# Both head pairs of a narrow score step in one unit, and maximum units of the first row block packed into the third's banks

## The chip, the cores and the metric

The kernel runs on one core of a Trainium2 chip. The metric is the device time of that core in microseconds (us). TensorE is called PE here, VectorE DVE, ScalarE ACT, GpSimd POOL, SyncE SP; PEld is PE's weight load, which the profile lists as a row of its own.

## The reference

One decoder layer with a post-layernorm, on x of 4 batches x 1,024 tokens x 256 channels, 16 heads of 16 channels:

```
x = layernorm(x + causal_self_attention(x))            # q, k, v, o with biases; softmax(q k^T / 4)
x = layernorm(x + cross_attention(x, ctx, mask))        # 64 keys per batch
x = layernorm(x + bitlinear_ffn(x))                     # 1,024 hidden, silu(gate) * up, down;
                                                        # activations to 8 bits, weights to -1, 0, 1
```

The change touches the causal self-attention alone: the scores of each head (queries x keys, keys up to the query's own), their row maximum, and the exponentials.

## The kernel before, in words

**Tiling.** The 1,024 queries of a batch fall into two column blocks c = 0 and 1 of 512 queries, the 16 heads into four groups g of four heads, and a group into two pairs p. The two heads of a pair lie in rows 0 to 63 and 64 to 127 of q_stack and k_stack (float16, each value split into a high and a low part), so that PE multiplies them at the same time. Each of the two writes a PSUM bank of 512 floats per partition. There are eight banks: bank 7 sums the outputs, and banks 0 to 6 are lent to units of work.

**Maximum units** (max_unit on PE, take_max on DVE). Before the exponentials the row maximum of the scores is taken: for a row block of 128 queries (qb, eight per batch, four per column block) PE multiplies queries by keys up to the diagonal, adds minus 1e30 above the diagonal with small matmuls of causal and pick_h, and DVE reduces both banks to the maximum. In column block 0 a (batch, c, g) has six units: row block 0 (128 keys, both pairs side by side in a bank), row block 1 (256 keys, both pairs), row block 2 (384 keys, a unit for each pair) and row block 3 (512 keys, a unit for each pair). Column block 1 has eight units of 512 earlier keys and then the same six. Over 4 batches and 4 groups these are 320 units. After the last one DVE makes the shift of that (c, g), which SP writes as a further row into q_stack.

**Score steps** (scores on PE, exponentials on ACT). A step is one (c, g) and one block kb of 128 keys, now with keys on the partitions and queries along the columns. Steps on the diagonal leave out the queries before their keys, and so have 512, 384, 256 and 128 queries; the others have 512. Every step is two units, one for each pair: two matmuls into two banks, and one exponential of ACT from both banks into probs. There are 192 steps and 384 such units; 32 steps have 256 queries and 32 have 128. On the diagonal POOL then zeroes the upper triangle (the "causal" step, line 727), and PE multiplies probs by v_aug (outputs, line 1069), 8 matmuls a step, into bank 7.

**What sets the order.** All five engines walk one list, `order`, which is spelled out by hand in the string ORDER: a letter takes the next unit of a chain and the digits behind it name the banks it gets. a is a score unit (or a causal step), m a maximum unit, o an output step, r projections, p, h, u and v what comes after the attention (output projection, cross-attention, feed-forward), z a "stir", four filler matmuls of PE. Each engine does its part of the units strictly in this order. A unit's PE part begins with free(u), which waits until the units that last had these banks have been read. When its last matmul ends it raises a semaphore (scores_ready, max_scores, unit_ready), on which the reader waits. probs_ready is raised by ACT, and max_taken by DVE. In this text a *unit boundary* is the place in PE's queue between the last matmul of a unit and the first of the next.

**Lines.** 1031 and 1038 are the score and the mask matmuls of a maximum unit, 1054 those of a score unit, 1069 the output step, 1175 the exponential, 1434 the maximum on DVE, 848, 861 and 928 float32 projections, 1001 and 1013 the feed-forward, 812 the stirs.

Of the kernel before, what the change touches and what calls it, by code (L numbers as in the profile page):

```python
# [15 lines left out]
P = 128  # L16
# [34 lines left out]
    "rr6r0r1ssr2r3r6r0sgsggr6swm01m23m45m01m23z6fm45gr6z1m12m45z3z6fm01m23r6a45m01m23fr6m45fa01fw2ffw3aa45a01w6aa"  # L51
    "45a23am01a45m23a56m01aa56fm23oa01fm45om23aa01z6m45a01m23fowoowm01m45m23sr6m45m01aa23a23aa56m23m01ggo45r6m23m"
    "01oa34aa56a23m01som56a34m12ooom56a34z0xz0m01o23xa56ffoa01m23m45sz6a01m23z6a56m01oa23m56a01oaa23m45m01a23am56"
    "owm23m01a56oga34m56aa12oa01aa23w6m45m01m56m34oowoa01z2z5a56o34a01oa56m23a01om56a23a01om23a45z6m01z6m56m34wz2"
    "a01az5z6a56a34az1z2a56a01oraa23a01m56m34aa12oa56am01oa23m45r6a01aooa34m56z2oa01aa34z2go01m23m45r6rm23m01r4m5"
    "6a23aa01oa34am56om01a23ooom45a23m01arz6z6m23m45wa01r6a01aa45o23om01m56a23oz4aa01em23ogogm45orm01a23r6o01a23m"
    "45obm01p23z5z5a01a45m23p6m45m23a01p6a23a01prm45r6m01em23oz5m01a45opp23m01m45rz6m01m23p6m01a45m23p6pp4p1p2p3g"
    "poaca45a01ap6z2p2p3p4a56a01agoa23a56aa01p4oa23p04a23r6p01p24m01rr6rbp01p23p45m01z6z3p45a23p01z6z6m34p56m01oo"
    "om23m45m01p6p3o01a45oa23a01pm45pr6m01a23m45oa01m23a56oppaa01z2a45am23om01ppa45a23rr6m45aa23p01om23a01aa45p6p"
    "0p1gm45m23oooom45m23p0p1p6p4p5p1p0pa23ar4a01pppp5p6z2o01a45aa23oga45pm01pppap23p6r4a01a56m23aa01a45p6opaa01a"  # L60
    "23z6ppm45pp01p6p3p2pz6z5gm01aa45a23apr6m23a45pa01pop45m01p6p23m45m01oop6p4o23axa01a56ooppa01m34p56ooom01m23m"
    "45p6m01a23p4pa01a23o56ota01oa34m01m56ooa01m23pp56m01m23m45ep6m23m01xa45p6pm45aa01a23p6p0p1gp4paa23a56aom23a0"
    "1a56ap4a01p5a23p6p4om23a01p6oooa45p02z6rr4r6p01p24rr6p01p45p23o01oa56p01p23oa01m45p23z6m01m45p6m45a01m23rp6p"
    "a45a01om56a34aom01m23a56pom56a01m23z4aa01a56aa01a23aa56pa01am23oom45m23ppa01pr6m45m01a23p56oom23m01aa45p6z2b"
    "m23gm45p0p1p6m23m01m45p6p2p3p0rp6o12a45p3pr0aa45a23apppp1p6m45ga23a01ppooooam01m45oa23rr6ro01ppp23p5p6pa01aa"
    "23a45oaa23a01pppm45m23p01p6p4p5paa01a23oooogpppm01m45p23p6o01om23p45p6m01a23a45p6ppp0p1a45a23p6p45om23m45a01"
    "p6p3a12a45r0ppm12m56a34om01aa34om34a01p56om01m23aa45p6m01m45m23p6pp4a01ap5a23p6a01p4gpaa23m01oa45m23a01p6p4p"
    "5a23ooop6a01a23o45p6om45p02rm45om45p01p24r6p01p23gp45m01a23p45p01a23rm56p01m23om45a01m23p6m01p4pm23a01aa56r4"
    "m01a56paoa23a01m56otappea01a23aa56a01m23pproom45m01aa23r6a45m23p01om45m23m01p6r4m23m01p6p4ap5p2p6m34m01p5ggo"
    "p2p3p4a56o01oopa01aa23a45appxpp6p0a23a45bppr6ppp01m23p4p6oooaa23a01pppm45r6o01app23p4p6p5pa34a01oaa23a56aa01"  # L70
    "ppm23gm45pop01p6m23m45p01p6m23a01p4ppp56a23tooxom01m45p6m23a01p4a23o01a56ppoa01m23a56om01a56a23aroa01a56om23"
# [14 lines left out]
    "6h0hooobh6h3oo01h6h3u01v56h3u4uuh05v4vu23h01h24vu6h01h23h45uu0u1v23h45uu6u1h23v0u6h23u05vv4v2h3u04vv2v6h3v6v"  # L86
    "05u23v05hu23u01hhv23hu56v12v34u6hhuuv01h56v0vh1h0uh4vvuuh3h6h2h1h0h5uh4u34hhhhh5h0hu3u1u5hvu6u0u4vhhh23h5h0v"
    "v56uuuhhuu3hhh12h5h0h4u3v5v2v0v4hhhhuv6v3h01h4uvuuh23u01vvvv6v2vu56vvh4h3vv56hu4u1uv56v3hv4z5z2vuz4z2z4z1z4z"
    "5z0z6z3vz0tttz2z4z1"
)  # L90


# [1424 lines left out]
```

## Time and profile before

| | us |
|---|---|
| median of 3 runs (lowest, highest) | 836.62 (831.83, 839.51) |
| the profiled execution | 836.75 |
| its span in the profile | 835.0 |
| PE matmuls busy | 787.4 (94%) |
| DVE busy | 682.5 (82%) |
| ACT busy | 575.8 (69%) |
| POOL busy | 347.6 (42%) |

Busy time is the union of an engine's instructions. A matmul's duration holds its passage through the array besides its columns, and matmuls overlap in it. So the start of the next matmul, not the end of this one, tells what a matmul costs PE. The spaces between columns that are shorter than this passage don't show as idle time. "issue" in the chain of waits is time in which the engine waited for nothing that the profile shows.

### The profile page before, as it was taken

The page shows a single profiled execution, that of the slowest core. Times are in us where ns is not written, and L with a number is a line of the kernel's source. Part 1 is how long each engine was busy: PE and PEld are TensorE (multiplying, and loading weights), DVE is VectorE, ACT ScalarE, POOL GpSimd, SP SyncE. Part 2 cuts the span into 40 slices and gives each one's busy share as a digit, 9 for nine tenths or more (in the row PEclk, how much of TensorE's full clock was granted, in tenths as well). Part 3 has the DMA queues.
Part 4 walks back from the last instruction along what each step waited for, and adds up shares of the span by engine and source line. Part 5 has one row for each costly group of instructions (what it writes and reads, how often), then busy time and mean ns, then how long its engine had stood idle before and what let it go on. Part 6 is the DMA issues. An engine that isn't in the chain of part 4 may idle for free.

```text
span 835.0 us, 20197 instructions
## 1 busy us (share of the span) xinstructions
PE 787.4 (94%) x7444; PEld 387.5 (46%) x7470; DVE 682.5 (82%) x1254; ACT 575.8 (69%) x753; POOL 347.6 (42%) x587
## 2 busy tenths in 40 slices
PE   8889999999999999999999999999999999999878
PEld 6534444354553435434553444544435343545536
DVE  6989998678987899868999589984999759745597
ACT  2457865559856598565876769765796589865495
POOL 5744355333433255423454153551525222652244
PEclk9989999999999999999999999999999999999899
DMA  6433002100212011011022010011101000000001
GB/s 191 125 103 98 2 20 66 54 18 17 67 36 64 1 33 28 3 38 51 13 73 77 1 48 19 8 35 50 46 2 37 11 1 26 26 28 1 2 1 53
DMA packets 37235, 32.86 MB, mean 39 GB/s; under 512 B 9828, under 2 KB 33348, under 8 KB 37140
## 3 DMA queue, kind: packets, MB, share of 16 engines
q1 hardware_dynamic: 33796, 28.89, 12.4%
q0 software_dynamic: 1440, 1.48, 0.8%
q10 hardware_dynamic: 1904, 1.18, 0.6%
q8 instruction: 64, 1.05, 0.6%
q14 instruction: 31, 0.25, 0.1%
HBM read 14.55 MB, written 4.19 MB: 22 GB/s over the span
## 4 chain that ended last, share of the span: by engine, by line
PE 65%; DVE 16%; ACT 9%; issue 6%; POOL 4%; DMA 0%; ACTq 0%; POOLq 0%; DVEq 0%
PE ps L1069 11%; PE ps L848 9%; PE ps L1054 7%; PE ps L1031 6%; DVE shift L1434 6%; PE ps L861 6%; PE ps L928 3%; ACT probs L1175 3%; PE ps L1001 3%; PE ps L1013 2%; PE ps L812 2%; PE ps L958 2%; PE ps L970 2%; PE ps L837 2%; PE ps L953 2%
## 5 line engine op out<-in xcount | busy, mean ns | idle before, releaser
L1175 ACT ACTIVATE probs<-ps 128x1024 f32<-128x1024 f32 (+3 forms) x384 | 294.7, 810 | 120.8 <-PE ps L1054 118.7
L1434 DVE TENSOR_REDUCE shift<-ps 128x2 f32<-128x1024 f32 (+2 forms) x320 | 343.5, 1112 | 42.1 <-PE ps L1031 20.7
L1069 PE MATMUL ps<-probs,v_aug 128*32 128x512 f32 (+3 forms) x1536 | 157.8, 501 | 0.0
L727 POOL TENSOR_SCALAR_AFFINE_SELECT probs<-probs 128x512 f32<-128x512 f32 x128 | 80.2, 637 | 157.9 <-ACT probs L1175 155.5
L1054 PE MATMUL ps<-q_stack,k_stack 49*128 49x512 f16 (+3 forms) x768 | 116.7, 328 | 12.0 <-ACT probs L1175 4.3
L1031 PE MATMUL ps<-k_stack,q_stack 48*128 48x512 f16 (+3 forms) x768 | 112.2, 329 | 9.8 <-DVE shift L1434 4.4
L1054 PEld LDWEIGHTS ps<-q_stack,k_stack 49*128 49x128 f16 x768 | 38.8, 93 | 106.5 <-ACT probs L1175 40.5
L1031 PEld LDWEIGHTS ps<-k_stack,q_stack 48*128 48x128 f16 x768 | 36.1, 94 | 98.4 <-ACT probs L1175 34.8
L1069 PEld LDWEIGHTS ps<-probs,v_aug 128*32 128x32 f32 x1536 | 35.3, 108 | 37.5 <-issue 26.7
L1310 DVE TENSOR_REDUCE shift<-ps 128x8 bf16<-128x512 f32 x64 | 40.1, 683 | 14.2 <-PE ps L939 14.0
L1257 DVE RECIPROCAL rden<-ps 128x16 f32<-128x16 f32 x64 | 16.1, 252 | 41.9 <-PE ps L837 41.5
L1038 PE MATMUL ps<-causal,pick_h 64*128 64x64 bf16 (+1 forms) x768 | 47.6, 198 | 0.0
L787 POOL TENSOR_SCALAR xt<-xt,mean_off,rstd 128x256 f32<-128x256 f32 x84 | 45.5, 554 | 2.3
L779 POOL TENSOR_SCALAR mean_off<-mv 128x4 f32<-128x4 f32 x21 | 4.1, 196 | 100.5 <-DVE mv L1356 100.4
L1038 PEld LDWEIGHTS ps<-causal,pick_h 64*128 64x128 bf16 x768 | 37.9, 95 | 12.9 <-issue 0.5
L1116 ACT ACTIVATE full<-ps,bias_scaled,kq_scale 128x512 f32<-128x512 f32 x30 | 23.4, 780 | 28.5 <-PE ps L861 20.8
L706 POOL CAST part_sb<-full 128x512 f16<-128x512 f32 x28 | 17.0, 609 | 59.8 <-ACT full L1116 59.7
L1307 DVE TENSOR_TENSOR xt<-ps,xt 128x512 f32<-128x512 f32 x32 | 22.0, 688 | 18.7 <-PE ps L848 18.3
L1332 DVE SCALAR_TENSOR_TENSOR region<-ps,dq_u,region 128x512 f32<-128x512 f32 x48 | 33.9, 745 | 1.0 <-PE ps L1001 0.8
L1346 DVE BATCH_NORM_STATS2 stats<-xt 128x6 f32<-128x256 f32 x96 | 34.0, 414 | 0.8
L1134 ACT ACTIVATE region<-ps 128x1024 f32<-128x1024 f32 x24 | 23.3, 1021 | 15.8 <-PE ps L958 15.8
L708 POOL TENSOR_TENSOR part_sb<-full,part_sb 128x512 f16<-128x512 f32 x28 | 32.4, 1157 | 2.3
(241 smaller groups left out, 1372.7 us busy)
## 6 DMA issues: line engine op xcount, KB each, us to landing
q_stack<-part_sb SPq DMA_DIRECT2D x164, 32.0 KB, 2.0
k_stack<-part_sb SPq DMA_DIRECT2D x147, 32.0 KB, 2.0
xT<-in_x_cols SPq DMA_DIRECT2D x8, 512.0 KB, 4.6
xt<-in_x SPq DMA_DIRECT2D x8, 512.0 KB, 3.6
out_x<-xt SPq DMA_DIRECT2D x7, 512.0 KB, 3.0
q_stack<-shiftT SPq DMA_DIRECT2D x128, 1.0 KB
k_stack<-part_sb POOLq DMA_DIRECT2D x45, 32.0 KB, 2.2
region<-in_w_gate SPq DMA_DIRECT2D x4, 256.0 KB, 3.8
```

Of the source, the lines that this page charges most:

```text
L727: pool.affine_select(out=blk, in_=blk, compare_op=ALU.is_ge, fill=0.0, base=0, pattern=[[0, HG], [1, P]], channel_multiplier=-1).then_inc( ...
L787: pool.tensor_scalar(xt[:, t, :], xt[:, t, :], mean_off[:, t:t + 1], rstd[:, t:t + 1], ALU.add, ALU.mult).then_inc(normed, 1)
L848: mm = pe.matmul(ps[:, u.bank, i * C:(i + 1) * C], src[:, d, i * P:(i + 1) * P], w[:, d, :], start=(d == 0), stop=(d == CC - 1))
L861: mm = pe.matmul(ps[:, u.bank, :], (wk, wq)[t][:, d, e * P:(e + 1) * P], xT[:, h, d, :], start=(d == 0), stop=(d == CC - 1))
L1031: mm = pe.matmul(ps[:, u.banks[s], j * w:(j + 1) * w], q_stack[at, u.b % 2, c, h, qb % TH * P:(qb % TH + 1) * P], k_stack[at, u.b % 2, h, ...
L1038: mm = pe.matmul(ps[:, u.banks[s], 0:n * w].rearrange("p (j w) -> p j w", j=n)[:, :, to], pick_h[rows, at], causal[rows, keys].unsqueeze(1 ...
L1054: mm = pe.matmul(ps[:, u.banks[i], 0:BANK - off], k_stack[at, b % 2, h, kb * P:(kb + 1) * P], q_stack[at, b % 2, c, h, off:BANK], start=Tr ...
L1069: mm = pe.matmul(ps[DV * i:DV * (i + 1), SUM_BANK, off:BANK], v_aug[:, kb, at:at + DV], probs_of(b, n)[:, i, :], start=first, stop=last)
L1175: act.activation(probs_of(b, n)[:, 2 * p:2 * p + 2, :], pair(u)[:, :, 0:BANK - off], ACT.Exp, scale=exp_scale).then_inc(probs_ready, 1)
L1310: ins = dve.tensor_reduce(shift2[:, t, e * HC:(e + 1) * HC], ps[:, k, :].rearrange("p (h k) -> p h k", k=TK), AX.X, ALU.max, negate=True)
L1346: ins = dve.bn_stats(stats[:, t, :], xt[:, t, :])
L1434: dve.tensor_reduce(to[:, :, pairs[0]:pairs[-1] + 1, qb % TH], pair(u)[:, :, 0:len(pairs) * w].rearrange("p j (h w) -> p j h w", w=w), AX. ...
```

## The change

Three edits. (1) A score step of 256 or 128 queries becomes one unit: its four matmuls write both pairs side by side into the two banks, and ACT takes them in one exponential. The 32 steps of 256 and the 32 of 128 queries have one unit in place of two, so the score units are 320 where they were 384. The counts of the semaphores stay as they were: such a unit raises scores_ready and probs_ready by two. (2) The maximum unit of the first row block of a column block (128 keys) is dropped; its two pairs are put behind the two pairs of the third row block (384 keys), which leave 128 columns of their banks free. The second row block comes first, the third with the first next, the fourth last. A column block thus has five such units in place of six (288 units where there were 320). DVE takes a packed unit with two reductions, since they have different widths and targets; the two mask matmuls of such a unit and row half reach over both parts. (3) ORDER is written anew: 1,885 entries in place of 1,981; the filler units are 56 in both.

```diff
--- before.py
+++ after.py
@@ -48,45 +48,42 @@
 PARTS, LAST_PARTS = [(0, 4), (4, 4)], [(0, 4), (4, 2), (6, 2)]
 
 ORDER = (
...
 )
 
 
@@ -172,17 +169,31 @@
             at += size
 
 
-    max_units = {0: [], 1: []}
-    for qb in range(TB):
-        w = (qb + 1) * P
-        c, k0 = qb // TH, qb // TH * BANK
-        n = min(BANK // (w - k0), HG // 2)
-        if c > 0:
-            max_units[c] += [(qb, 0, BANK, [p], False) for p in range(HG // 2)]
-        max_units[c] += [(qb, k0, w - k0, list(range(p, p + n)), True) for p in range(0, HG // 2, n)]
+    max_units = {}
+    for c in range(QC):
+        t0 = c * TH
+
+        def diagonal(t, pairs, at):
+            return [(t0 + t, c * BANK, (t + 1) * P, p, True, at + n * (t + 1) * P) for n, p in enumerate(pairs)]
+
+        max_units[c] = [[(t0 + t, 0, BANK, p, False, 0)] for t in range(TH if c > 0 else 0) for p in range(HG // 2)]
+        max_units[c] += [diagonal(1, [0, 1], 0)]
+        max_units[c] += [diagonal(2, [p], 0) + diagonal(0, [p], 3 * P) for p in range(HG // 2)]
+        max_units[c] += [diagonal(3, [p], 0) for p in range(HG // 2)]
+
+    def reductions(unit):
+
+        same = {}
+        for piece in unit:
+            same.setdefault(piece[0], []).append(piece)
+        return list(same.values())
 
     def maxima(b, c, g):
         return [Unit("max", b, (c, g, i), "dve") for i in range(len(max_units[c]))]
+
+    def score_pairs(b, n):
+
+        return [[0, 1]] if BANK - steps[b][n][3] <= BANK // 2 else [[0], [1]]
 
     def crossing():
         return [Unit("maskin", 0, 0)]
@@ -266,7 +277,7 @@
               "f": [Unit("ffn_load", 0, (n, i)) for n in range(3) for i in range(QUARTERS)], "h": [], "x": [], "e": [], "b": [], "c": [], "t": [], "u": [], "v": [], "z": [Unit("stir", 0, n) for n in range(STIRS)]}
     for b in range(NB):
         for n, (g, c, kb, off, diag, begins, ends) in enumerate(steps[b]):
-            chains["a"] += [Unit("scores", b, (n, 0)), Unit("scores", b, (n, 1))] + ([Unit("causal", b, n)] if diag else [])
+            chains["a"] += [Unit("scores", b, (n, pairs[-1])) for pairs in score_pairs(b, n)] + ([Unit("causal", b, n)] if diag else [])
             chains["o"] += [Unit("pv", b, n)] + ([Unit("o_copy", b, n), Unit("turn", b, (c, g), "dve")] if ends else [])
         for c, g in GROUP_ORDER if b < NB - 1 else LAST_ORDER:
             chains["m"] += maxima(b, c, g)
@@ -1016,44 +1027,53 @@
 
             def max_unit(u):
                 c, g, i = u.idx
-                qb, k0, w, pairs, diag = max_units[c][i]
+                unit = max_units[c][i]
                 free(u)
                 if (u.b, i) == (0, 0):
                     pe.wait_ge(consts_ready, 1)
                 if i == 0:
                     for n in (2 * c, 2 * c + 1):
                         wait_moved(pe, u.b, g, n)
-                n = len(pairs)
-                for j, p in enumerate(pairs):
+                masked = unit[0][4]
+                for n, (qb, k0, w, p, diag, to) in enumerate(unit):
                     h = g * HG // 2 + p
                     for s, rows in enumerate(four):
                         at = slice(rows.start, rows.start + SH)
-                        mm = pe.matmul(ps[:, u.banks[s], j * w:(j + 1) * w], q_stack[at, u.b % 2, c, h, qb % TH * P:(qb % TH + 1) * P],
-                                       k_stack[at, u.b % 2, h, k0:k0 + w], start=j == 0 or not diag, stop=not diag)
-                if diag:
+                        mm = pe.matmul(ps[:, u.banks[s], to:to + w], q_stack[at, u.b % 2, c, h, qb % TH * P:(qb % TH + 1) * P],
+                                       k_stack[at, u.b % 2, h, k0:k0 + w], start=n == 0, stop=not masked)
+                if masked:
+                    ends = [to + w for qb, k0, w, p, diag, to in unit]
+                    n, apart = len(unit), ends[-1] - ends[0]
                     for part in range(2):
                         at, keys = slice(part * P, (part + 1) * P), slice(part * HALF, (part + 1) * HALF)
-                        to = slice(w - P + part * HALF, w - HALF + part * HALF)
+                        first = ends[0] - P + part * HALF
                         for s, rows in enumerate(four):
-                            mm = pe.matmul(ps[:, u.banks[s], 0:n * w].rearrange("p (j w) -> p j w", j=n)[:, :, to], pick_h[rows, at],
-                                           causal[rows, keys].unsqueeze(1).broadcast_to([HALF, n, HALF]), start=False, stop=part == 1)
+                            if n == 1:
+                                to, which = ps[:, u.banks[s], first:first + HALF], causal[rows, keys]
+                            else:
+                                to = ps[:, u.banks[s], ends[1] - 2 * apart:ends[1]].rearrange("p (j w) -> p j w", j=2)
+                                to = to[:, :, apart - P + part * HALF:apart - HALF + part * HALF]
+                                which = causal[rows, keys].unsqueeze(1).broadcast_to([HALF, n, HALF])
+                            mm = pe.matmul(to, pick_h[rows, at], which, start=False, stop=part == 1)
                 mm.then_inc(max_scores, 1)
 
             def scores(u):
                 b, (n, pair) = u.b, u.idx
                 g, c, kb, off, diag, first, last = steps[b][n]
+                w, pairs = BANK - off, next(some for some in score_pairs(b, n) if some[-1] == pair)
                 free(u)
                 if first and pair == 0:
                     s = shift_of[b, c, g]
                     pe.wait_ge(shift_loaded[s % 2], 16 * HG * (s // 2 + 1))
                 if (b, n, pair) == (0, 0, 0):
                     pe.wait_ge(ones_moved, 32)
-                h = g * HG // 2 + pair
-                for i, rows in enumerate(four):
-                    at = slice(rows.start, rows.start + SH + 1)
-                    mm = pe.matmul(ps[:, u.banks[i], 0:BANK - off], k_stack[at, b % 2, h, kb * P:(kb + 1) * P],
-                                   q_stack[at, b % 2, c, h, off:BANK], start=True, stop=True)
-                mm.then_inc(scores_ready, 1)
+                for j, p in enumerate(pairs):
+                    h = g * HG // 2 + p
+                    for i, rows in enumerate(four):
+                        at = slice(rows.start, rows.start + SH + 1)
+                        mm = pe.matmul(ps[:, u.banks[i], j * w:(j + 1) * w], k_stack[at, b % 2, h, kb * P:(kb + 1) * P],
+                                       q_stack[at, b % 2, c, h, off:BANK], start=True, stop=True)
+                mm.then_inc(scores_ready, len(pairs))
 
             def outputs(b, n):
                 g, c, kb, off, diag, first, last = steps[b][n]
@@ -1170,10 +1190,16 @@
                 if (n, p) == (0, 0):
                     act.wait_ge(unscale_ready, b + 1)
                     act.reg_load(exp_scale, unscale[0:1, b:b + 1].bitcast(I32))
-                if p == 0 and probs_over[b, n] is not None:
+                pairs = next(some for some in score_pairs(b, n) if some[-1] == p)
+                m, w = len(pairs), BANK - off
+                if pairs[0] == 0 and probs_over[b, n] is not None:
                     act.wait_ge(pv_done, probs_over[b, n] + 1)
-                act.activation(probs_of(b, n)[:, 2 * p:2 * p + 2, :],
-                               pair(u)[:, :, 0:BANK - off], ACT.Exp, scale=exp_scale).then_inc(probs_ready, 1)
+                if m == 1:
+                    to, src = probs_of(b, n)[:, 2 * p:2 * p + 2, :], pair(u)[:, :, 0:w]
+                else:
+                    to = probs_of(b, n).rearrange("p (j s) q -> p j s q", s=2)
+                    src = pair(u)[:, :, 0:m * w].rearrange("p s (j q) -> p j s q", j=m)
+                act.activation(to, src, ACT.Exp, scale=exp_scale).then_inc(probs_ready, m)
 
             exp_scale = act.alloc_register("exp_scale")
             act.dma_start(wk[:], Wk.rearrange("(c p) n -> p c n", p=P)).then_inc(kq_loaded[1], 16)
@@ -1426,14 +1452,17 @@
 
             def take_max(u):
                 c, g, i = u.idx
-                qb, k0, w, pairs, diag = max_units[c][i]
+                unit = max_units[c][i]
                 first = shift[:, c, g, :, :].rearrange("p k (j h t) -> p k j h t", j=2, t=TH)
                 dve.wait_ge(max_scores, u.ready)
                 m = shift_of[u.b, c, g]
-                to = first[:, k0 // BANK]
-                dve.tensor_reduce(to[:, :, pairs[0]:pairs[-1] + 1, qb % TH],
-                                  pair(u)[:, :, 0:len(pairs) * w].rearrange("p j (h w) -> p j h w", w=w),
-                                  AX.X, ALU.max, negate=True).then_inc(max_taken, 1)
+                for group in reductions(unit):
+                    qb, k0, w, p, diag, at = group[0]
+                    n = len(group)
+                    ins = dve.tensor_reduce(first[:, k0 // BANK, :, p:p + n, qb % TH],
+                                            pair(u)[:, :, at:at + n * w].rearrange("p j (h w) -> p j h w", w=w),
+                                            AX.X, ALU.max, negate=True)
+                ins.then_inc(max_taken, 1)
                 if i == len(max_units[c]) - 1:
                     dve.wait_ge(max_taken, u.taken)
                     if c > 0:
```

## Rows read from the trace of the kernel before

**Rows 1.** The page: engines' busy time, clock by slice.

```profile
PE 787.4 (94%) x7444; PEld 387.5 (46%) x7470; DVE 682.5 (82%) x1254; ACT 575.8 (69%) x753; POOL 347.6 (42%) x587
...
PEclk9989999999999999999999999999999999999899
```

**Rows 2.** Stretches: length, then busy us (count) of PE, PEld, DVE, ACT, POOL; clock.

```profile
20.00:100.00 80.00, 71.61 (x683) 33.71 (x682) 72.06 (x98) 53.47 (x66) 40.08 (x67) 0.96 0.31 87
100.00:200.00 100.00, 97.29 (x891) 45.41 (x890) 81.38 (x135) 61.32 (x81) 47.63 (x72) 1.00 0.13 33
...
600.00:700.00 100.00, 93.73 (x908) 42.46 (x912) 82.08 (x142) 78.30 (x103) 35.20 (x60) 1.00 0.06 16
...
760.00:835.00 75.00, 62.66 (x652) 39.58 (x648) 55.52 (x149) 47.29 (x68) 28.09 (x51) 0.95 0.05 16
```

**Rows 3.** The page: chain of waits, by engine and by line.

```profile
PE 65%; DVE 16%; ACT 9%; issue 6%; POOL 4%; DMA 0%; ACTq 0%; POOLq 0%; DVEq 0%
PE ps L1069 11%; PE ps L848 9%; PE ps L1054 7%; PE ps L1031 6%; DVE shift L1434 6%; PE ps L861 6%; PE ps L928 3%; ACT probs L1175 3%; PE ps L1001 3%; PE ps L1013 2%; PE ps L812 2%; PE ps L958 2%; PE ps L970 2%; PE ps L837 2%; PE ps L953 2%
```

**Rows 4.** Groups by line and shape, PE: busy us, mean ns | idle before.

```profile
L1054 PEld LDWEIGHTS ps<-q_stack,k_stack 49*128 49x128 f16 x768 | 38.8, 93 | 106.5 <-ACT probs L1175 40.5 <-issue 23.0 <-DVE shift L1434 22.4
...
L1054 PE MATMUL ps<-q_stack,k_stack 49*128 49x128 f16 x128 | 12.8, 220 | 1.8 <-ACT probs L1175 1.4
```

**Rows 5.** Timeline of PE at four places: start, length, instructions.

```profile
305.63 1.90 PE L1001 MATMUL ps<-gateT,region 128*128 128x512 bf16 x8
...
158.68 0.39 PE L1054 MATMUL ps<-q_stack,k_stack 49*128 49x256 f16 x4
159.00 0.64 PE L1069 MATMUL ps<-probs,v_aug 128*32 128x512 f32 x4
...
224.24 0.43 PE L1054 MATMUL ps<-q_stack,k_stack 49*128 49x128 f16 x4
224.60 0.42 PE L1069 MATMUL ps<-probs,v_aug 128*32 128x256 f32 x4
...
310.75 0.43 PE L1054 MATMUL ps<-q_stack,k_stack 49*128 49x128 f16 x4
311.12 0.39 PE L1001 MATMUL ps<-upT,region 128*128 128x512 bf16 x1
```

**Rows 6.** Timeline of the weight loads at two of these places.

```profile
158.67 0.11 PEld L1054 LDWEIGHTS ps<-q_stack,k_stack 49*128 49x128 f16 x4 [0.21 <-ACT probs L1175]
...
310.72 0.33 PEld L1054 LDWEIGHTS ps<-q_stack,k_stack 49*128 49x128 f16 x4 [0.81 <-ACT probs L1175]
```

**Rows 7.** Groups by line and shape, maxima on DVE.

```profile
L1434 DVE TENSOR_REDUCE shift<-ps 128x2 f32<-128x768 f32 x64 | 59.6, 952 | 5.5 <-PE ps L1038 5.2
...
L1434 DVE TENSOR_REDUCE shift<-ps 128x4 f32<-128x1024 f32 x32 | 39.0, 1218 | 1.7 <-PE ps L1038 1.7
...
L1434 DVE TENSOR_REDUCE shift<-ps 128x4 f32<-128x512 f32 x32 | 21.7, 679 | 4.0 <-PE ps L1038 3.7
```

**Rows 8.** Groups by line and shape, exponentials on ACT.

```profile
L1175 ACT ACTIVATE probs<-ps 128x1024 f32<-128x1024 f32 x192 | 189.5, 1023 | 79.5 <-PE ps L1054 78.2 <-issue 0.2
...
L1175 ACT ACTIVATE probs<-ps 128x512 f32<-128x512 f32 x64 | 36.4, 598 | 13.3 <-PE ps L1054 13.0
...
L1175 ACT ACTIVATE probs<-ps 128x256 f32<-128x256 f32 x64 | 22.4, 382 | 9.4 <-PE ps L1054 8.9
```

**Rows 9.** The page: costliest groups, exponentials and maxima in all.

```profile
L1175 ACT ACTIVATE probs<-ps 128x1024 f32<-128x1024 f32 (+3 forms) x384 | 294.7, 810 | 120.8 <-PE ps L1054 118.7
L1434 DVE TENSOR_REDUCE shift<-ps 128x2 f32<-128x1024 f32 (+2 forms) x320 | 343.5, 1112 | 42.1 <-PE ps L1031 20.7
```

**Rows 10.** Waits: who for whom, us in total, times, longest.

```profile
ACT probs L1175 <- PE ps L1054: 118.7, 140, 6.5
...
PEld ps L1054 <- ACT probs L1175: 40.5, 70, 1.2
PEld ps L1031 <- ACT probs L1175: 34.8, 63, 0.9
```

More of the change, by code:

```diff
@@ L56 @@
[L56 to L60, printed above, removed]
@@ L86 @@
[L86 to L89, printed above, removed]
+    "rr6r0r1ssr2r3r6r0sgsggr6swm23m45m01m23z6z5z5m45fffffgm01z6r6z4z5m45m01r6fa45m01m23r6m45a01w2w3z6faa45a01aw6f"
+    "fffa45am23m56m01a34awom23a45sofm01z6z6m23owa01awm45m23z6m56z4a01m23z4a45m01aooa23m45r6o01m23ggsom01m45r6m01a"
@@ new lines @@
+    "a23oaa56a34m01m56z2a23m01oosom56a34w2o01goa56m23a01m56m23a01oa56m01a34om56a01aa23z4z4m01m56a34om34m01om56aa3"
+    "4aoa12aa34m01m56m34woa01ooxz5z5a56a01o34oa56m23z0xa01m56a34a12m56om01m23z5z4wa56oa01am23a45oa01aa34ara56az2z"
+    "0z0m56m23a01oa45m01oaa23m56r4a01oooaa45gz6o01am23m45r6rm23m01r4m56a23aa01oa23m45om01aa23m56a34m01raoom23z4wo"
+    "em45a01r6o23m01om45gaa23oaa01oorga23om45bm01r6o23m01a45om23p56m01z4a34rp6a45a01m23p6pz0m45a23a01r6m01m23om01"
+    "a45gpop23m45z1m01m23p6m01a45m23p6pp0p2p3gp4paa56a01aop5rp2p3p4a01aa56oaa01a23p5op04a23r6rp01p24m01r6p01p23p4"
@@ new lines @@
+    "5m01z6z6p56a23p01z4z4gm23p56m01ooorm23m45p6m12p0a34o56oa23pa01m45pr6a23m45oa01m23a45poaa01m23a56opz1ppm01m45"
+    "gaa23arr6p23a01aa45om23p6p0p1m45m23ooop4om56m23p1p0p4p5p1p6pa23er4aa01pppp5p6z2o01a23aa45gaopm01pppp23p5r4a5"
+    "6aa01m23p6pa45aa01a23oom56pppp01p4p3p2paa45appr6m23m01pp45p6a23om45op23m01ap6p4o23ba01a56xppoa01p23m45ooom01"
+    "m45a23gop6m12p4a01a23po56oa01oa23m01m45ooa23m01pp56z4m34m01p6m23m01a45p6pp5am34a01p2p5p6pa01oaa34m12z5aa56ap"
+    "3p0a56p2p4z3z1xm56a23a01p4ooroa56p03r5r6op01p24rr6rp01p45gp23o01oa56p12p34oa01m56p23m01m45p6m45m23a01p6pa01a"
@@ new lines @@
+    "23a45om01pz2atm23a45a01m56m34ppaa12coaa01aa56oppm23m45a01r6m23oaa01m45oa23m01p45m23oom01p6z5m23m45gp0p1p2ap3"
+    "m01m45p6p3p2rp0p1a56ao34r0a23appppp1p6rm45a23a01oooapppom01m45oa23r6po01rp45p3p2pa01aa34aa56opppp01am23p5p4p"
+    "6a23oa45pm01ooeopppp23m45gp6o01om23p45p6m01a23a45p6pa23bpp0p1p6a23p45om23a01p5p0a34ptpa56m12r0m56a34om12m34a"
+    "a56oa01p56om01m34p6m01m45m23p6pp4p5aa01p3p6poaa45m01aa23a45p6m23a01ooop4p5a23a01p6o45ga23p6om56p02m56oz4p01p"
+    "24rr6p01p23p45m01ra23p56p01a23m45p01m23m56m01p4p5a34a12appr6m01m23a45oa45am01ocm56a23opaa01agpa45m23opa01pam"
@@ new lines @@
+    "45rr6a23a45om01p23om56m23om01p4r5m23m01p4p6p5p3p2p6m01p5p3p2aa01o56paa34oopppap2p1a34a56ppar0m34ggppp12p6p0e"
+    "ooom45a23pr6a01o23pppp45p0p6p1xaa23aa45apoa01m23m45pppoobp01p3m45p01p6m23a45p1ppxp23oom01m45a23p6m23a01p4a23"
+    "o01ppa56om23a01a45om01a56a23roaa01a56om23p01m45om23m01p6m23m45p1pp6ap0a23p1p6pam45a23op6gp2aa01a45p3p6oa01m2"
+    "3a45p6om01or2p35r2o01p56p02p45rr6a01p23p45m23a01op45a23p01a56m23p01om34p6m23m01ra45p6pa45aa23r0pm34m56gga12a"
+    "om34a01toaa56aa12m34a56oaa23ppm01a45ppoom45m23aa01rr6m23p01om56rm23op4gp0p1p6m23m45p0p1o23m56p4p1p2aa56ap4m0"
@@ L90 @@
+    "3a56aooa23h01a56aa23oh1aa34h6hh5h3h0h1oaohooh6h0o34h5h6u01v45h6bu3uuh05v4vvu23h01h24u6uh01h23h45u0u1v23h56uu"
+    "4u0h23v1vu6h23u05v4v2h3vv2v6u04h3v2v05u34v15hhu34u12v34hu56v12v34u5uhhv01hh56uv3vh4h2h6uz5vh5uuuh0h4h1h3vh6h"
+    "2u56hhhhh1h4vhu5u1u6u3u2hhvhu4h01h6h3vv01uuhhhhh56uuh3h0u2v4h3u1v6v4huv1v2v3hhhh01uh6h01vvuuvvv2v4vu01u56vh2"
+    "h4vhu1u2vuv56v34v1v5hz1z1z0z6vuz6z4z0z2z5z5vz1z1z2tttz0"
 )
```

40 lines of the change are left out of this document (10 added, 30 removed).

## The prediction, made before the change was run

> **What bounds the kernel now.** I read the page's busy times first: PE is busy for 94% of the span, DVE for 82%, ACT for 69%, and PE's clock is at its upper level, 2.4 GHz, nearly throughout [rows 1]. Then the stretches, since an average hides different limits [rows 2]. From 100 to 200 us PE is idle for 2.7 us, from 600 to 700 us for 6.3 us. From 20 to 100 us it is idle for 8.4 us while DVE is busy for 72 of 80: there the maxima of the first batch bound the kernel. The last 75 us, where the attention is over, have 12.3 us of idle time, and no unit of the change lies there. The chain of waits says the same [rows 3]: 65% on PE, 16% on DVE, of which 6 points are maxima (L1434), 9% on ACT, of which 3 are exponentials (L1175). So what counts is time on PE's queue, and nearly every us saved there between 100 and 740 us is a us of the kernel. An engine beside it counts for the small share with which it stands in the chain.
>
> **What a unit costs PE.** The change takes no column from PE, so I ask what a unit costs beside its columns. Eight matmuls of 512 columns in a row take 1.90 us; less the 0.39 us that a single one lasts, seven starts take 1.51 us, 0.216 us each, or 0.054 us for 128 columns [rows 5]. The two matmuls of a pair run at the same time. Two units of 128 queries therefore have 0.11 us of columns, but from the start of the first to the next unit's start it is 0.36 us at 224.24 and 0.37 us at 310.75. Two units of 256 queries at 158.68 have 0.22 us of columns and take 0.32 us [rows 5]. The surplus is 0.25, 0.26 and 0.10 us over two unit boundaries, 0.13, 0.13 and 0.05 us each. The weight loads say why [rows 6]: at 310.72 the four loads are spread over 0.33 us, since the second unit's loads begin after its wait, and one load takes 93 ns [rows 4]; at 158.67 all four fit in 0.11 us, the second unit's wait was over early, and that boundary is free. A boundary thus costs one exposed weight load or none. I take the mean of the three places, 0.10 us.
>
> The Trainium skill has a rule against this (TensorE: Matmul & The Clock Gate, the introductory table and Part 3): PE's queue is 64 deep and pulls weight loads ahead of matmuls in flight. Taken alone it would hide every boundary, and the saving on PE would be zero. The trace agrees at one of the three places and contradicts it at two.
>
> **The change, part by part.**
>
> (1) One unit per narrow score step. 64 boundaries go from PE: 64 x 0.10 = 6.4 us. The bounds are 0.05 and 0.13 us each, 3.2 to 8.3 us. On ACT the 32 steps of 256 queries need one exponential of 1,024 elements in place of two of 512, 1,023 against 2 x 598 ns, and the 32 of 128 queries one of 512 in place of two of 256, 598 against 2 x 382 ns [rows 8]. That is 32 x (173 + 166) ns = 10.8 us less of ACT's 575.8. ACT is not the bound: exponentials stand with 3% of 835 us = 25 us in the chain, out of 294.7 us busy [rows 3, 9]. So 25/295 = 8.5% of a change on ACT reaches the end: 0.9 us less. The consumers don't get later by themselves: POOL's causal step and the output step waited for both pairs before, too. The bank pair is held longer by one exponential, which I cost at nothing, covered by the other two pairs of banks; without that cover it is the slower rival.
>
> (2) The first row block's unit goes. Per (batch, c, g) six units become five, 32 boundaries, 32 x 0.10 = 3.2 us (1.6 to 4.2). The mask columns on PE are the same: before, two units with 128-column masks and four with 64, four matmuls each; after, three and two, 2,048 columns both ways. 128 weight loads and mask matmuls fewer run beside other work, at nothing. DVE pays: in place of one reduction of 512 elements (679 ns) there are two of 256. That shape is not in the trace; 512, 768 and 1,024 elements take 679, 952 and 1,218 ns [rows 7], 0.27 us per 256, so 256 takes 679 - 270 = about 0.41 us. Two are 0.82, so 0.14 us more, times 32 = 4.5 us on DVE. Its floor is no cost, if PE always bounds; its ceiling all 4.5 us. Maxima stand in the chain with 6% of 835 = 50 us out of 343.5 busy [rows 3, 9], 15%: 0.7 us more. SP's load of the shift row hangs on the last unit of the (c, g) as before; with one unit fewer ahead of it on PE it is not later.
>
> (3) The new order. Its chains, the fillers (56) and the pattern of banks are of the same kind. Each queue is walked in the new order, SP's and POOL's too: residual loads, moves of the pieces and stores stand elsewhere, but these engines are idle most of the time (POOL 42% busy), and DMA has 0% of the chain. The waits that the order makes can't be read from the trace of before. I take zero; the ends are given by PE's idle time outside the tail, 47.6 - 12.3 = 35.3 us [rows 1, 2]: a third less is 11.8 us gained, half more is 17.6 us lost.
>
> The sum, against the profiled execution of 836.75 us (0.13 above the median of 836.62): -6.4 - 3.2 - 0.9 + 0.7 = -9.8, so **827 us**. In the first 100 us DVE binds, and a few of the 96 boundaries there are worth less; against that stands the load that they take off the banks. I leave both out.
>
> **Rivals.** *Nothing gained.* Every boundary is in truth hidden, or PE stands that much longer at the next wait for a reader: 836.75 + 0.7 - 0.9 = 836.6. For it speaks that PE's weight loads stood idle 75 us until exponentials were done [rows 10]: some boundaries coincide with real waits, and then the saving is only moved. Against it: these are 133 waits in all, and the matmuls of the 128-query steps have only 1.8 us of PE's idle time before them [rows 4]. Here also falls the case that what the change saves is used up by DVE: 4.5 us in full leaves 831.
>
> *More gained.* 96 of 704 attention units, 14%, no longer ask for banks, and the new order uses this: a third of the 35.3 us of idle time goes too, 827 - 11.8 = 815.
>
> *Slower.* A merged unit keeps both banks until an exponential of 1,023 ns is over where 598 did, and 598 where 382 did. If PE, at lines 1031 and 1054, has no other pair free at that time, the difference falls on it: 32 x (425 + 216) ns = 20.5 us, and the end is 836.75 - 9.8 + 20.5 = 847.5. It decides (over 1% slower) from 18.2 us on, when nearly nine tenths of it are exposed. For it: ACT's exponentials already end many waits of PE's weight loads [rows 10]. Against it: ACT itself waited 118.7 us for score matmuls [rows 10], so it is mostly ahead, and its load falls. A worse order, by half more idle time, would come to the same figure, 845.
>
> **How the numbers follow.** Forecast 0.42, nothing gained 0.21, more gained 0.19, slower 0.18. The forecast's own range by the boundary prices (4.8 to 12.5 us instead of 9.6) is 824 to 832, widened by small shifts of the order to 821 to 834. The whole range reaches to the rivals on both sides: 813 to 845. A measurement of this kernel can tell about 1% from no change, 8.4 us: faster is under 828.3. Of the forecast's 0.42 I put 0.26 under that and 0.16 above; with the case of more gained, faster is 0.45. The same is 0.16 + 0.21 less 0.01, and the slower case lies partly inside 1%: same 0.37, slower 0.18.
>
> **What would show it.** The maxima are 352 reductions in 288 units, with 64 of 256 elements in the packed units near 0.41 us, DVE's maxima some 4 us up. Exponentials are 320, about 284 us. Mask matmuls are 640. PE's idle time outside the tail stays near 35 us, and the gain from 100 to 740 us comes with fewer boundaries, not with fewer columns: the chain's share of L1054 falls. The forecast is wrong if PE's idle time moves by more than 10 us either way, or if waits of lines 1031 and 1054 for ACT rise while its busy time falls; then the order or the longer hold decides, and not the boundaries.

## The result: 2 to 3 us faster, under a third of what was forecast

Over 20 runs each the median fell from 834.87 to 832.84 us; the ratio of the runs is 0.9966, 95% interval 0.9951 to 0.9981, so -2.8 us (-4.1 to -1.6). I had forecast 827 us, -9.8 us. One of the changed kernel's 20 runs took 1,051 us at a mean granted clock of 0.65 and is left out of the ratio. The time lies in my range, but the size is off by more than three times, and it falls within 1% of no change, where I had put 0.37.

One correction first: I described column block 1 of the kernel before as eight unmasked maximum units "and then the same six". As its code (lines 176 to 182) shows, they alternate there: of each row block first its two unmasked units, then its masked ones. All eight first is the changed kernel's doing; an experiment below tries it.

The page of the kernel after: busy times and clock, then the chain of waits by engine and by line.

```profile
PE 779.4 (94%) x7342; PEld 380.8 (46%) x7342; DVE 682.6 (82%) x1286; ACT 569.6 (69%) x689; POOL 347.4 (42%) x587
...
PEclk9999999999999999999999999999999999999999
...
PE 57%; DVE 26%; ACT 8%; issue 6%; POOL 2%; DMA 0%; ACTq 0%; POOLq 0%; DVEq 0%
DVE shift L1462 13%; PE ps L1089 10%; PE ps L859 8%; PE ps L1042 6%; PE ps L872 6%; PE ps L1074 6%; PE ps L939 3%; ACT probs L1202 3%; PE ps L1012 2%; PE ps L969 2%; DVE amax L1412 2%; PE ps L981 2%; PE ps L964 2%; PE ps L823 2%; PE ps L848 2%
```

Against [rows 1, 3]: PE's busy time fell by 8.0 us, nearly what I had summed, and the span of this execution by 7.1 us. But it ran at a mean granted clock of 0.996, the one of before at 0.988 (and the trace of before lacks 26 matmul records, 7,444 beside 7,470 weight loads). The 61 runs of before that were made beside the experiments give 623 us per unit of mean clock (835.9 us at 0.990, 830.8 at 0.998). So 0.008 of clock is 5.0 us, and 2.1 us are left, about as in the medians. One profiled execution against another would have come near my forecast by chance. In the chain the maxima on DVE went from 6 to 13%.

The same stretches of the kernel after as in [rows 2], with the same columns:

```profile
20.00:100.00 80.00, 72.63 (x686) 33.60 (x684) 75.21 (x108) 53.49 (x59) 42.78 (x71) 1.00 0.31 88
100.00:200.00 100.00, 96.83 (x881) 43.67 (x878) 81.57 (x140) 62.77 (x76) 42.67 (x64) 1.00 0.13 31
...
600.00:700.00 100.00, 92.89 (x901) 41.78 (x898) 82.45 (x146) 77.97 (x93) 32.10 (x56) 1.00 0.07 20
```

PE idles 3.2 us where it idled 2.7, and 7.1 where it idled 6.3, and 48.5 us in all where it idled 47.6. That is too little to build on: the stretches don't hold quite the same work, and records are missing.

The starts in the two traces say more. For every run of score matmuls of one width I take the time from its first start to the start of the next other instruction, less its columns at 0.216 us per 512, and call the rest surplus. At the steps of 256 and 128 queries the surplus is 17.4 us in all before and 8.0 after. So their boundaries did give 9.4 us back in PE's queue, even more than the 6.4 forecast. But at the steps of 512 and 384 queries, which the change leaves alone, the surplus rose from 26.2 to 30.2 us: 4.0 us came back there.

Groups of the kernel after by line and shape, against [rows 4, 7, 8]:

```profile
L1202 ACT ACTIVATE probs<-ps 128x1024 f32<-128x1024 f32 x224 | 222.2, 1023 | 89.9 <-PE ps L1074 86.3 <-issue 2.1
...
L1462 DVE TENSOR_REDUCE shift<-ps 128x2 f32<-128x768 f32 x64 | 61.0, 953 | 5.5 <-PE ps L1057 5.0
...
L1057 PE MATMUL ps<-causal,pick_h 64*128 64x128 bf16 x384 | 27.1, 215 | 0.0
L1462 DVE TENSOR_REDUCE shift<-ps 128x2 f32<-128x256 f32 x64 | 26.7, 417 | 0.0
...
L1202 ACT ACTIVATE probs<-ps 128x512 f32<-128x512 f32 x32 | 19.2, 599 | 9.8 <-PE ps L1074 9.6
```

The durations are as forecast: merged exponentials of 1,023 and 599 ns, reductions of 256 elements at 417 ns (0.41 forecast). Their sums are not what the engines' busy time changed by, since instructions that follow at once overlap: at 309.45 two reductions of 953 and 417 ns are done after 1.28 us. The maxima's busy time rose by 0.8 us where I expected some 4 (343.5 to 344.3; all of DVE 682.5 to 682.6), and ACT's fell by 6.2 us where I had 10.8.

The signs I had named are mixed. PE's idle time outside the tail is 36.3 us, near 35, and the counts of instructions are as forecast. The waits of weight loads for exponentials, 75 us before [rows 10], fell to 58; those for maxima at the maximum units rose from 24.3 us to 33.2:

```profile
PEld ps L1042 <- DVE shift L1462: 33.2, 62, 1.1
PEld ps L1074 <- ACT probs L1202: 31.5, 52, 1.3
PEld ps L1042 <- ACT probs L1202: 26.6, 49, 0.9
```

What failed is what a us on each engine is worth.

### The profile page after: what moved, and what is told of

Read it like the earlier page. It is cut to its first block, busy times and chain, and to the rows that moved or that the text cites. A ratio compares the mean times of both kernels' runs of the same rounds, so it can differ in the third digit from the quotient of the medians.

```text
span 827.9 us, 19835 instructions
## 1 busy us (share of the span) xinstructions
PE 779.4 (94%) x7342; PEld 380.8 (46%) x7342; DVE 682.6 (82%) x1286; ACT 569.6 (69%) x689; POOL 347.4 (42%) x587
## 3 DMA queue, kind: packets, MB, share of 16 engines
q8 instruction: 62, 1.02, 0.5%
## 4 chain that ended last, share of the span: by engine, by line
PE 57%; DVE 26%; ACT 8%; issue 6%; POOL 2%; DMA 0%; ACTq 0%; POOLq 0%; DVEq 0%
DVE shift L1462 13%; PE ps L1089 10%; PE ps L859 8%; PE ps L1042 6%; PE ps L872 6%; PE ps L1074 6%; PE ps L939 3%; ACT probs L1202 3%; PE ps L1012 2%; PE ps L969 2%; DVE amax L1412 2%; PE ps L981 2%; PE ps L964 2%; PE ps L823 2%; PE ps L848 2%
## 5 line engine op out<-in xcount | busy, mean ns | idle before, releaser
L1462 DVE TENSOR_REDUCE shift<-ps 128x2 f32<-128x1024 f32 (+3 forms) x352 | 344.3, 1024 | 35.4 <-PE ps L1042 18.0
L1202 ACT ACTIVATE probs<-ps 128x1024 f32<-128x1024 f32 (+1 forms) x320 | 287.6, 938 | 114.2 <-PE ps L1074 110.1
L1074 PE MATMUL ps<-q_stack,k_stack 49*128 49x512 f16 (+3 forms) x768 | 109.1, 327 | 10.0 <-DVE shift L1462 3.1
L1042 PE MATMUL ps<-k_stack,q_stack 48*128 48x512 f16 (+3 forms) x768 | 107.2, 327 | 11.3 <-DVE shift L1462 4.0
L1074 PEld LDWEIGHTS ps<-q_stack,k_stack 49*128 49x128 f16 x768 | 35.2, 93 | 98.4 <-ACT probs L1202 31.5
L1042 PEld LDWEIGHTS ps<-k_stack,q_stack 48*128 48x128 f16 x768 | 33.1, 94 | 98.8 <-DVE shift L1462 33.2
L1057 PE MATMUL ps<-causal,pick_h 64*128 64x128 bf16 (+1 forms) x640 | 41.8, 205 | 0.0
L1333 DVE TENSOR_TENSOR xt<-ps,xt 128x512 f32<-128x512 f32 x32 | 22.0, 688 | 19.9 <-PE ps L859 19.8
L1057 PEld LDWEIGHTS ps<-causal,pick_h 64*128 64x128 bf16 x640 | 29.9, 95 | 11.7
```

Source lines behind the costliest of these rows:

```text
L1042: mm = pe.matmul(ps[:, u.banks[s], to:to + w], q_stack[at, u.b % 2, c, h, qb % TH * P:(qb % TH + 1) * P], k_stack[at, u.b % 2, h, k0:k0 + ...
L1057: mm = pe.matmul(to, pick_h[rows, at], which, start=False, stop=part == 1)
L1074: mm = pe.matmul(ps[:, u.banks[i], j * w:(j + 1) * w], k_stack[at, b % 2, h, kb * P:(kb + 1) * P], q_stack[at, b % 2, c, h, off:BANK], sta ...
L1202: act.activation(to, src, ACT.Exp, scale=exp_scale).then_inc(probs_ready, m)
L1462: ins = dve.tensor_reduce(first[:, k0 // BANK, :, p:p + n, qb % TH], pair(u)[:, :, at:at + n * w].rearrange("p j (h w) -> p j h w", w=w), ...
```

## The experiments

All were timed in five rounds beside the kernel before; a difference in us is the ratio's part of 834.9 us. "Over the changed kernel" counts from the changed kernel's place, 2.8 us under before. Diffs in this section are in outline.

The medians mix in the clock. The last column gives each run's distance from the kernel before at the same mean clock, by the line through the 61 runs of before (623 us per unit; they lie within 0.8 us of it). The clock may itself follow from an edit, if it makes PE wait, so the truth about an edit can lie between the columns.

| run | over before, us | mean clock | at the same clock, us |
|---|---|---|---|
| the changed kernel | -2.8 | 0.992 | -2.4 |
| both_old_order | +17.7 | 0.987 | +14.8 |
| scores_old_order | +7.6 | 0.991 | +7.4 |
| max_old_order | +8.9 | 0.993 | +9.6 |
| boundaries_back | -5.3 | 0.995 | -3.0 |
| exps_apart | -2.0 | 0.993 | -2.6 |
| dve_more | +14.4 | 0.993 | +12.7 |
| dve_more_before | +19.8 | 0.985 | +15.8 |
| dve_less | -7.2 | 0.993 | -6.4 |
| pe_more | +1.3 | 0.994 | +2.3 |
| max_old_interleaved | +14.6 | 0.991 | +11.4 |
| scores_old_late | +17.2 | 0.985 | +10.4 |
| before_moved | +19.9 | 0.984 | +15.6 |
| before_three_moved | +4.9 | 0.989 | +4.3 |
| scores_apart_new_order | +65.9 | 0.969 | +52.8 |

**Each edit in the old order.** `both_old_order`, `scores_old_order` and `max_old_order` keep the list of before, with entries struck out where units vanished:

```diff
-aXY aUV            (a step of 256 or 128 queries)
+aXY                (both pairs)
-mXY mUV ...        (first row block, second row block, ...)
+mUV ...            (second row block first)
```

> Both structural edits in the order of before: of each narrow score step the second entry of a is struck out, of each (batch, c, g) the entry of m that was the first row block's; all other entries and their banks stay. Theory A (a unit boundary is worth about 0.10 us wherever it is taken away, and the new order gave the saving back): 8 to 10 us faster than before. Theory B (PE stands at the next wait for a reader instead, whatever the order): within 3 us of before, as the changed kernel is (-2 us). Theory C (merging costs, because both banks are held through a longer exponential and the order was laid for short ones; the new order had to repair that): slower than before by 2 to 10 us.

> Only the score steps merged, in the order of before with the second entry of a struck out of each narrow step. Theory A: -7.3 us (64 boundaries at 0.10 and 0.9 us by ACT). Theory B: within 2 us of before. Theory C: slower by 1 to 8 us.

> Only the maximum units packed, in the order of before with one entry of m struck out of each (batch, c, g). In column block 1 this also puts the eight unmasked units ahead of the masked ones, as the change does. Theory A: -2.5 us (32 boundaries at 0.10, DVE +0.7). Theory B: within 2 us. Theory D (the 4.5 us more on DVE stand in the path in full, since PE waits for maxima): +1 to +4 us.

Measured: both 852.19 us, 1.0212 (1.0184 to 1.0239), +17.7 us; scores alone 841.91 us, 1.0091 (1.0065 to 1.0118), +7.6 us; maxima alone 843.55 us, 1.0107 (1.0076 to 1.0137), +8.9 us (a later expectation has 8.2, the difference of the medians). The direction is theory C's, and the score edit's size too; both together lie above its 2 to 10 us, and the maxima above theory D's 1 to 4. The two roughly add up. With entries merely struck out the change would have cost 18 us; the list written anew is worth about 20 us against that. Where the score edit loses, in the stretches from 200 and from 300 us of scores_old_order (before: PE busy 96.86 and 96.32), and its waits for exponentials (the longest single one before: 0.9 us at the maximum units, 1.2 at the score units, [rows 10]):

```profile
200.00:300.00 100.00, 94.86 (x891) 46.34 (x894) 83.41 (x154) 66.15 (x79) 34.28 (x57) 0.97 0.14 39
300.00:400.00 100.00, 92.11 (x899) 43.02 (x900) 84.22 (x150) 68.14 (x79) 38.72 (x62) 1.00 0.12 31
```

```profile
PEld ps L1033 <- ACT probs L1186: 38.3, 61, 2.1
PEld ps L1058 <- ACT probs L1186: 36.3, 54, 1.5
...
PE ps L1058 <- ACT probs L1186: 9.0, 18, 1.3
```

PE's idle time proper before score matmuls, until exponentials were done, is 9.0 us where it was 4.3, and before those of maximum units 5.4 where it was 1.5. By the starts, the score units are not where the time goes: the surplus of the narrow ones fell here too, from 17.4 to 11.1 us, and that of the wide ones rose by 0.8. The matmuls of maximum units take 118.7 us of PE's queue where they took 112.6. That fits merged units which keep a pair of banks through an exponential of 1.02 us while the list goes on asking for that pair. It is not shown to be the cause: the controls below lose as much with nothing merged.

**The boundary by itself.** `boundaries_back`:

```diff
 for j, p in enumerate(pairs):
+    if j > 0:
+        pe.wait_ge(pool_ready, 2)
```

and the same once per (batch, c, g) in a packed maximum unit.

> The changed kernel in its own order, but with 96 waits that are always satisfied put back on PE: between the two pairs of each merged score unit and between the two parts of one packed maximum unit per (batch, c, g). Nothing else differs. If a boundary is the wait in PE's queue and costs 0.10 us each on the path: 9.6 us slower than the changed kernel, so 842 us. If a satisfied wait lets the weights be loaded early, or PE would have stood at the next reader anyway: under 2 us slower than the changed kernel.

Measured: 829.73 us, 0.9936 (0.9912 to 0.996), not slower than the changed kernel but 2.5 us below it, with intervals that overlap; at the same clock 0.6 us are left of the 2.5. 96 satisfied waits cost nothing that can be measured, and the surplus of the narrow steps stays at 8.5 us (8.0 without them). PE's timeline at the same place, first the changed kernel, then this one:

```profile
304.70 0.39 PE L1074 MATMUL ps<-q_stack,k_stack 49*128 49x256 f16 x4
304.93 0.41 PE L848 MATMUL ps<-ident,o_sb 64*128 64x64 f32 x8
```

```profile
304.58 0.39 PE L1078 MATMUL ps<-q_stack,k_stack 49*128 49x256 f16 x4
304.81 0.41 PE L848 MATMUL ps<-ident,o_sb 64*128 64x64 f32 x8
```

0.23 us from start to next start with or without the wait, for 0.22 us of columns; two separate units took 0.32 us at 158.68 [rows 5]. So the surplus that I read there is not the price of a wait instruction. The run doesn't put back what else a boundary had, a bank pair that a reader may not have let go yet, and a signal.

The trace of before tells which it was. In 38 of its 64 narrow steps the two units stand side by side. At 17 of them the second unit's matmuls follow the first's columns within 0.03 us, on average 0.01, as inside the merged units (0.01 us with or without the added wait). At the other 21 the gap is 0.06 to 1.27 us, and at 14 of these the last semaphore that the second unit's load waited for came 0.105 us before the load. So a boundary is free where the reader is done early, and costs what is left of the wait where it isn't. The 38 gaps sum to 5.9 us.

**ACT's share.** `exps_apart`:

```diff
-act.activation(both pairs).then_inc(probs_ready, 2)
+act.activation(pair 0).then_inc(probs_ready, 1)
+act.activation(pair 1).then_inc(probs_ready, 1)
```

> The changed kernel in its own order; only ACT takes each merged score unit with two exponentials, as before the change (598 + 598 ns for 1,023, 382 + 382 for 598; 10.8 us more on ACT, and both banks kept 0.17 us longer). My prediction prices it at 0.9 us over the changed kernel, by the exponentials' 3% of the chain. If the length for which a bank pair is kept is what the order hangs on: 3 to 11 us over the changed kernel.

Measured: 831.17 us, 0.9976 (0.9951 to 1.0002), 0.8 us over the changed kernel, but at the same clock 0.1 us under it. My 0.9 us can't be told from zero here. By the page the 10.8 us of longer exponentials raise ACT's busy time by 3.4 us only (569.6 to 573.0). Banks held 0.17 us longer in 64 units don't show.

**DVE's share, up, down, and in the kernel before.**

```diff
 (dve_more)        + dve.tensor_reduce(extra[...], the same 256 elements, ...)
 (dve_more_before) + the same two reductions ahead of the first row block's
 (dve_less)        - the reductions of 256 elements
```

> The changed kernel with each of its 64 reductions of 256 elements done once more into a place that nobody reads (26.7 us more on DVE, and the packed units' banks kept 0.42 us longer). By the 15% that I took from the chain: +4 us over the changed kernel. If DVE's maxima are a bound of their own, as the chain of the changed kernel says (13% of the span for them, 6% before): +13 us or more.

> The kernel before with the same 64 extra reductions of 256 elements on its first row blocks' units (26.7 us more on DVE), results unread. In the changed kernel this cost 17 us, 0.64 us per us. If DVE passes its time on in the kernel before as well, and my 15% from the chain was wrong from the start: 13 to 20 us over before. If it became a bound only through the change: 4 to 8 us over before.

> The changed kernel without its 64 reductions of 256 elements (26.7 us less on DVE); the first row block's maxima are left out and its shift is zero. If DVE's time counts the same way down as up: 15 us or more faster than the changed kernel, about 816 us. If the order as written, PE and ACT hold the time once DVE is quicker: under 6 us faster.

Measured: dve_more 846.16 us, 1.0172 (1.014 to 1.0204), 17.2 us over the changed kernel, 0.64 per us of DVE. dve_more_before 855.41 us, 1.0237 (1.0211 to 1.0262), 19.8 us over before, 0.74 per us. dve_less 826.71 us, 0.9914 (0.9885 to 0.9942), 4.3 us under the changed kernel, 0.16 per us. At the same clock the three prices are 0.57, 0.59 and 0.15. The 26.7 us are a sum of durations that overlap: DVE's busy time changed by +18.5, +20.2 and -19.5 us, and per us of that the prices are 0.93, 0.98 and 0.22. DVE was so sensitive before the change, too, so the change didn't make it a bound. But it is lopsided: more work costs four times what less work gives. The added reductions also keep banks longer; the runs don't separate that from DVE's own time. In dve_more the view of waits shows the new ones:

```profile
PEld ps L1043 <- DVE shift L1463: 23.4, 44, 1.0
...
PEld ps L1043 <- DVE extra L1467: 15.3, 19, 1.8
```

19 waits of weight loads of up to 1.8 us for the extra reductions, where the longest wait there for a maximum was 1.1 us in the changed kernel.

**PE's share.** `pe_more`:

```diff
-for j, p in enumerate(pairs):
+for j, p in [*enumerate(pairs)] * len(pairs):
```

> The changed kernel with the four score matmuls of each of the 64 merged units done twice over the same columns (32 x 0.215 + 32 x 0.107 = 10.3 us more of columns on PE, no further wait). If PE's queue is the bound, as my prediction had it: 9 to 11 us over the changed kernel. If PE has slack between the waits for its readers: under 4 us over it.

Measured: 835.89 us, 1.0015 (1.0 to 1.003), 4.1 us over the changed kernel for 10.3 us of columns, 0.40 per us (at the same clock 4.7 us, 0.45): between the two expectations, and nearer to the second. At these places PE is not the bound that 94% busy made it look. Over the whole queue its time counts for more, by an estimate from the clock: an execution of before whose mean clock is 0.001 lower has 0.84 us less of full clock in its 835 us and takes 0.62 us longer, 0.75 per us.

**Packing and placing.** `max_old_interleaved` lists column block 1's units as before; `scores_old_late` strikes the first entry instead of the second.

```diff
 (max_old_interleaved)  for t in range(TH): two unmasked units of t, then the masked ones of t
 (scores_old_late)      -aXY ... aUV   +aUV at the second place
```

> As max_old_order (+8.2 us, 1.0107 of before), but the maximum units of column block 1 stand as in the kernel before: of each row block its two unmasked units and then its masked ones (row blocks 0 and 1: four unmasked, then the second's; then third with first; then fourth). If the eight unmasked units in a row (short on PE, 1.22 us each on DVE) are what costs: back to within 2 us of before. If it is the packing itself (the packed unit keeps its banks for two reductions, 0.95 + 0.42 us) or the struck entry: it stays at +6 to +10 us.

> As scores_old_order (+7.6 us, 1.0091 of before), but the first of the two entries of a narrow step is struck out and the merged unit stands at the place and on the banks of the second. If the loss came from which entry was struck (banks held while PE already asks for them): it goes to within 2 us of before. If any such order, laid for exponentials of 0.6 and 0.38 us, loses with ones of 1.02 and 0.6 us: +5 us or more again.

Measured: 845.74 us, 1.0175 (1.0146 to 1.0204), +14.6 us; and 850.24 us, 1.0206 (1.017 to 1.0242), +17.2 us. The eight unmasked units in a row are not what costs; alternating them costs 6 us more in this order, 2 us at the same clock. Between the two places of the merged unit lie 10 us, but 3 at the same clock: the mean clock of scores_old_late is 0.985 where that of scores_old_order is 0.991. Both places lose 7 us or more.

**Controls: nothing merged, entries moved.** The kernel before with the second entry of some narrow steps put right behind the first:

```diff
-aXY  other entries  aUV
+aXY aUV  other entries
```

> A control: the kernel before, nothing merged; in 19 of the 64 narrow steps, whose two entries don't stand side by side (and are on different banks), the second entry is moved to directly behind the first, with its own banks. scores_old_order has its merged units at these places and lost 7.6 us. If moving PE's and ACT's work forward in a finely laid order costs this by itself: +4 to +9 us. If the loss comes from the merging (one bank pair kept longer, the other left empty): within 2 us of before.

> As before_moved (19 entries moved, +20 us), with three of these 19 moves only, over 2, 5 and 5 places of the list. If the loss adds up move by move at 1 us each: +2 to +4 us. If one displaced entry upsets the order as a whole: +8 us or more. If a few moves are absorbed: within 1.5 us.

Measured: 19 moves 854.05 us, 1.0238 (1.0204 to 1.0272), +19.9 us; three moves 841.08 us, 1.0059 (1.0033 to 1.0086), +4.9 us. About 1 to 1.6 us a move, with no change to any unit; both losses lie above their expectations for a sum of moves (4 to 9 and 2 to 4 us). The loss shows at the moved units: the surplus of the narrow steps is 31.3 and 21.5 us where it was 17.4. So scores_old_order's loss says little of merging. Part of the loss goes with the clock, 15.6 us are left at the same one: the stretch from 20 us of before_moved has a mean clock of 0.89 (before: 0.96).

```profile
20.00:100.00 80.00, 71.43 (x641) 33.22 (x639) 68.24 (x95) 48.41 (x60) 39.15 (x67) 0.89 0.32 89
```

**From the other side.** `scores_apart_new_order` undoes the merging in the new order:

```diff
-aXY                (both pairs)
+aXY aUV            (UV: the pair of banks left alone longest)
```

> The inverse of scores_old_order: the changed kernel with its packed maximum units and its new order, but every narrow score step again as two units; the added entry stands directly behind the merged one, on the pair of banks that was left alone longest. If merging by itself is worth the 6.4 us of boundaries and 0.9 us of ACT that I gave it: 7 us over the changed kernel. If each order only fits its own set of units, so that any edit of the list loses: 7 us or more too, and then this run does not tell the two apart. Under 3 us over the changed kernel: merging is worth next to nothing, and this order is not fragile.

Measured: 902.54 us, 1.0789 (1.0756 to 1.0822), +66 us. I put it down to my insertions, which take a pair away from the next entries, but no run shows that: from 300 to 400 us PE is busy for 90.07 us.

```profile
300.00:400.00 100.00, 90.07 (x793) 39.06 (x791) 82.38 (x142) 65.51 (x85) 39.78 (x64) 0.95 0.11 31
```

As its expectation says, it doesn't tell the worth of merging from a list that no longer fits.

## Why the prediction was wrong

**Steps (1) and (2), 96 boundaries at 0.10 us, each counted in full at the end: the step that failed.** As a gap in PE's queue the price was not too high: the surplus at the 64 merged steps fell by 9.4 us, 0.15 us each, and in scores_old_order, with the order kept, by 6.3 us, my 0.10 each. What failed is "nearly every us saved there between 100 and 740 us is a us of the kernel". I summed 9.6 us, and the time fell by 2 to 3 in all. 4.0 us of surplus came back at the wide score units, and pe_more, which adds PE work at just these merged units, passes on 0.40 per us (0.45 at the same clock). At that price 9.6 us are about 4.

I also read wrongly what the gap is. The weight loads in [rows 6] had told me that it appears where "the second unit's loads begin after its wait", and that wait is one for a reader of the banks. boundaries_back put 96 satisfied waits back at no cost, where the expectation by my price was 9.6 us, and in the trace of before 14 of the 21 open gaps end right after a semaphore. So what a saved unit gives back is mostly what is left of a wait for a reader, and that wait may go to the next unit. The 4.0 us at the wide units are in line with this; no run shows it wait by wait. And I split each surplus over two boundaries, of which merging takes only the inner one: at 158.68 this one has 0.01 of the 0.10 us, at 224.24 and 310.75 it has 0.15 of 0.25.

The Trainium skill's rule that weight loads are pulled ahead in PE's queue, to other rows or to the background buffer (TensorE: Matmul & The Clock Gate, Part 3), which I weighed against two of three places, describes this run: with the wait satisfied the four loads take 0.11 us (at 304.57 of boundaries_back) and the matmuls 0.23 us from start to start.

**DVE at 15%: wrong in price and in amount.** The measured price of added work is 0.64 to 0.74 per us of duration, that of work left out 0.16. The amount, 4.5 us, was a sum of durations; the maxima's busy time rose by 0.8 us. At 0.93 per us of busy time that is 0.7 us, the figure I had, by luck: two errors that cancel.

**ACT at 0.9 us: not shown.** Exponentials taken apart cost between -0.1 us (at the same clock) and 0.8, and ACT's busy time fell by 6.2 us in place of 10.8.

**The new order at zero: wrong as a step, though by luck not far off in the sum.** In the old order, with entries struck out, the edits cost 17.7 us; the new list is worth that much and 2.8 us more. My slower rival, the longer hold, is not what the changed kernel shows: its weight loads wait less for exponentials, not more. Whether it is what costs in the old order is open, since 19 moved entries lose as much with nothing merged, and packing alone loses 8.9 us. The rival "nothing gained" is nearest to what happened, in its second form, in which PE stands that much longer at the next wait. It isn't that every boundary was hidden.

**What stays open.** What merging and packing are worth with a list laid for each. Moving three entries costs 4.9 us and moving 19 costs 19.9, so no run that edits the list isolates it. Nor is it shown where the rest of the 9.4 us went, beyond the 4.0 at the wide units. Known is that ACT's part is about 1 us or less, that satisfied waits cost nothing, and that all of it together with the list is 2 to 3 us.

## What to carry to other kernels

Before pricing a gap in one engine's queue as its cost, ask whether the instruction behind it waits for a reader: put a satisfied wait there, and look whether a semaphore arrived just before the instruction. If so, the gap is the reader's, and removing the unit may only move it. Then look at the gaps of the units that were left alone. In a kernel whose order is written out by hand, a chain's share is no price for added work; a doubled piece of work on each engine (here 0.64 on DVE, 0.40 on PE) is one for that place, and it can be four times larger upward than downward. A sum of durations overstates what an engine's busy time gains or loses when instructions follow at once. Judge a change of units only together with its order, and compare executions at the same granted clock.

## What the runs showed of the hardware

The mean granted clock of an execution differs from run to run of the same program, from 0.986 to 1.000 over 61 runs of the kernel before, and explains nearly all of their spread: the median is 838.6 us at 0.986, 835.9 at 0.990, 833.8 at 0.994, 830.8 at 0.998, 830.0 at 1.000. The changed kernel has a similar slope and lies 2 us lower (833.9 at 0.990). The spread of 1% that I took for noise is thus mostly TensorE falling to its lower level, 1.2 GHz, for some stretches and not others: in the kernel before the profiled execution had 0.96 from 20 to 100 us [rows 2], in the one after 1.00; in all they spent 20.5 and 6.8 us at the lower level.

Reductions on DVE that follow at once overlap. 64 added ones of 415 ns raised its busy time by 18.5 us in dve_more, 0.29 us each.
